# Ranking and writing back tokens in a modulated feed-forward stage: half-width comparisons, a bias put into PSUM by TensorE, residual rows summed on GpSimd

## The reference

```
def _L1_ffn_ref(x, attention_mask, wr, br, w1, b1, w2, b2):
    weights = (jnp.einsum('bsd,do->bso', x, wr) + br)[..., 0]
    k = max(1, int(CAPACITY * s))
    kk = k - 1 if k > 1 else 1
    _, idx = jax.lax.top_k(weights, k)
    sel_idx = idx[:, :kk]
    sel = jnp.take_along_axis(x, sel_idx[:, :, None], axis=1)
    h = jax.nn.gelu(jnp.einsum('bkd,dh->bkh', sel, w1) + b1)
    y = jnp.einsum('bkh,hd->bkd', h, w2) + b2
    w_sel = jnp.take_along_axis(weights, sel_idx, axis=1)
    y = y * w_sel[..., None]
    processed = jnp.zeros_like(x).at[batch_idx, sel_idx].set(y)
    return processed + x

x = x + _L1_ffn_ref(_layernorm(x, axis=-1), ...)
```

## Time and profile before

| | |
|---|---|
| time, median of 3 runs | 4688.07 us (4686.57 to 4688.72) |
| profiled execution, first to last instruction (its span) | 4591.2 us |
| the profiled execution's own time | not recorded apart from its span |
| TensorE matmul busy, share of the span | 3499.2 us, 76% |
| VectorE busy | 2854.1 us, 62% |
| ScalarE busy | 2105.7 us, 46% |
| GpSimd busy | 1802.9 us, 39% |
| the stage `mod_stage` in the span | 2499.3 us to 2699.1 us |

### The profile page before, as it was taken

The page is one execution under the profiler, slowest core; times in us unless marked ns, Lnnn a source line. Parts: engine busy times, 40 slices in busy tenths (PEclk is TensorE's granted clock), DMA queues, the critical chain, the costliest instruction groups (busy, mean ns, idle before and its releaser), DMA issues. The chain is left out here.

```text
span 4591.2 us, 80959 instructions
## 1 busy us (share of the span) xinstructions
PE 3499.2 (76%) x23827; PEld 2132.6 (46%) x23827; DVE 2854.1 (62%) x10855; ACT 2105.7 (46%) x5250; POOL 1802.9 (39%) x2183
## 2 busy tenths in 40 slices
PE   3999995666666638999987867639947788884994
PEld 1333333444444423333345656627736555553663
DVE  5666656555555567777758977832247677763444
ACT  1777773322222216777753236624426555551321
POOL 3555520000000015555456225855545525544444
PEclk8999995555555559999998988869969999996997
DMA  4334318600000014333300012225442000002445
GB/s 130 112 112 118 118 53 368 261 0 0 0 0 0 0 54 126 112 112 111 89 6 2 1 57 71 70 83 153 148 156 80 32 1 20 20 20 85 129 130 162
DMA packets 237349, 378.44 MB, mean 82 GB/s; under 512 B 24832, under 2 KB 157056, under 8 KB 228672
## 3 DMA queue, kind: packets, MB, share of 16 engines
q1 hardware_dynamic: 218688, 337.44, 23.3%
q0 software_dynamic: 18432, 38.31, 2.4%
HBM read 210.70 MB, written 164.95 MB: 82 GB/s over the span
## 5 line engine op out<-in xcount | busy, mean ns | idle before, releaser
L1461 DVE CUSTOM_DVE_ANT_0 mha_seen<-mha_score,mha_mask 128x512 f32<-128x512 f32 x1024 | 684.7, 688 | 378.9 <-PE mha_score L1216 372.9
L1360 ACT ACTIVATE mha_prob<-mha_turned 128x512 f32<-128x512 f32 x1024 | 589.6, 603 | 303.1 <-PE mha_turned L1230 295.9
L1617 PE MATMUL lstm_gates<-lstm_h_part,lstm_w_part 128*128 128x16 f16 x4608 | 277.6, 179 | 327.8 <-DVE lstm_h_part L1832 324.5
L3131 POOL DMA_INDIRECT expert_rows<-expert_y,expert_target x320 | 306.9, 959 | 359.5 <-DVE expert_y L3277 154.6
L1216 PE MATMUL mha_score<-mha_k_rows,mha_q_rows 96*128 96x512 bf16 x1024 | 397.9, 391 | 56.4 <-DMA mha_k_rows<-split_rows 29.5
L1617 PEld LDWEIGHTS lstm_gates<-lstm_h_part,lstm_w_part 128*128 128x128 f16 x4608 | 217.2, 107 | 480.2 <-DVE lstm_h_part L1832 475.5
L1230 PE MATMUL mha_turned<-mha_q_rows,mha_k_rows 99*128 99x512 bf16 x1024 | 389.9, 382 | 8.4 <-ACT mha_turned L1341 6.7
L1564 POOL TENSOR_TENSOR core_mid<-lstm_hist,lstm_per_unit 128x128 f32 x64 | 29.5, 461 | 886.7 <-DVE lstm_hist L1833 886.7
L1704 ACT ACTIVATE lstm_act<-lstm_gates 128x48 f32<-128x48 f32 x512 | 108.0, 211 | 428.6 <-PE lstm_gates L1617 428.6
L1229 PE MATMUL mha_turned<-mha_maskT,core_ident_bf 128*128 128x512 bf16 x768 | 294.8, 384 | 0.3
L3169 PEld LDWEIGHTS expert_out_ps<-expert_w,expert_hid 128*128 128x128 f32 (+1 forms) x2240 | 262.4, 191 | 38.7 <-issue 33.0
(11 more groups left out here) (553 smaller groups left out, 8960.9 us busy)
## 6 DMA issues: line engine op xcount, KB each, us to landing
routed_rows<-lstm_blank SPq DMA_DIRECT2D x66, 1056.0 KB, 27.0
core_params<-adj SPq DMA_DIRECT2D x32, 1024.0 KB, 5.9
gat_adj_raw<-adj SPq DMA_DIRECT2D x32, 1024.0 KB, 5.5
mha_q_rows<-split_rows SPq DMA_DIRECT2D x64, 384.0 KB, 5.3
mha_k_rows<-split_rows SPq DMA_DIRECT2D x64, 384.0 KB, 6.0
expert_x<-routed_rows SPq DMA_DIRECT2D x80, 264.0 KB, 2.8
expert_w<-weights SPq DMA_DIRECT2D x80, 256.0 KB, 3.6
combine_pair<-expert_rows SPq DMA_DIRECT2D x32, 512.0 KB, 4.9
```

The lines of the kernel that those rows point to most:

```text
L1360: act.activation(prob[:, n % RING, :], turned[n % 3][:, :], ACT.Exp, scale=-1.0).then_inc(S["prob_ready"], 1)
L1461: dve.tensor_tensor_reduce(seen[n % 2][:, :], score[n % 2][:, :], mask[1 - s][:, t, :], 1.0, 3e38, ALU.add, ALU.min, low[g][:, t, j:j + 1] ...
L1617: return pe.matmul(out, w[:, g * P:(g + 1) * P], h_part[:, part, :], start=False, stop=stop, skip_group_check=True)
L3131: pool.indirect_dma_start(out=core.y_rows[NUMBER][:, :], out_offset=bass.IndirectOffsetOnAxis(ap=target[q][:, t:t + 1], axis=0), in_=y_buf ...
```

## The change

It touches `mod_stage` alone, in four pieces.

1. The comparisons take only the columns that their mask can leave standing: `earlier` of tile t columns 0 to 128(t+1), `later` of tile t columns 128t to 512.
2. The bias no longer goes through VectorE. Once, at the start of the stage, VectorE cuts it into three bf16 parts that add up to it, and lays them on partitions 0, 32 and 64 of a tile that is otherwise zero (`cut_bias`). TensorE multiplies that tile by a tile of ones and so starts `out_ps` with the bias in all 512 columns; the output matmuls add to it.
3. GpSimd adds the residual rows to the normalised rows (`residual`, into two buffers `base`), as a third pass for each graph. VectorE takes output times coefficient plus `base` straight from `out_ps` into `core.x_res`. The operations into `y` and the sum in `write_x` are gone.
4. The waits that follow from it: `x_taken` (VectorE has taken a graph's output) takes the place of `out_taken`; `base_ready` is new; and TensorE waits for `bias_set` once, behind the first `spread` and ahead of the first hidden tile.

```
+            pool.memset(bias_ones[:, :], 1.0).then_inc(S["bias_set"], 1)
+            def residual(b, s):
+                pool.wait_ge(S["xn_ready"], b + 1)
+                if not isinstance(b, int) or b >= 2:
+                    pool.wait_ge(S["x_taken"], b - 1)
+                apart(pool, core)
+                pool.tensor_tensor(base[s][:, :, :], rows_.xn[b % 3][:, :, :], core.x_res[:, b], ALU.add).then_inc(S["base_ready"], 1)
+            def graph(b, s, first=False, last=False):
+                rows_.normalise(pool, b)
+                residual(b, s)
...
+                if b >= 2:
+                    pe.wait_ge(S["x_taken"], b - 1)
+                pe.matmul(out_ps[s][:, :], bias_ones[:, :], flat(bias_rows[:, :, :]), start=True, stop=False)
                 pe.wait_ge(S["hid_free"], H * (b + 1) + 3)
-                pe.wait_ge(S["out_taken"], b + 1)
...
             spread(0)
+            pe.wait_ge(S["bias_set"], 2)
             each_graph(pe, graph)
...
+            def cut_bias():
+                chain = Chain(dve, S["bias_chain"])
+                left = par("mb2")
+                chain.step(dve.memset(bias_rows[:, :, :], 0.0))
+                for i in range(3):
+                    chain.step(dve.tensor_copy(bias_cut[:, i, :], left))
+                    chain.settle()
+                    if i < 2:
+                        chain.step(dve.tensor_tensor(bias_left[:, :], left, bias_cut[:, i, :], ALU.subtract))
+                        chain.settle()
+                        left = bias_left[:, :]
+                for i in range(3):
+                    row = slice(32 * i, 32 * i + 1)
+                    chain.step(dve.tensor_copy(bias_rows[row, :, :], bias_cut[row, i, :].unsqueeze(1).broadcast_to([1, T, D])))
+                chain.settle()
+                dve.sem_inc(S["bias_set"], 1)
...
-                        chain.step(dve.scalar_tensor_tensor(hits[:, 2 * t + i, :], wrow[:, :], wcol[s][:, t:t + 1],
-                                                            tri[:, t, :], op, ALU.mult, accum_out=count[:, i, t:t + 1]))
+                        chain.step(dve.scalar_tensor_tensor(hits[:, 2 * t + i, lo:hi], wrow[:, lo:hi], wcol[s][:, t:t + 1],
+                                                            tri[:, t, lo:hi], op, ALU.mult, accum_out=count[:, i, t:t + 1]))
...
-                dve.tensor_tensor(y[:, :, :], out_ps[s][:, :].rearrange("p (t d) -> p t d", t=T),
-                                  par("mb2").unsqueeze(1).broadcast_to([P, T, D]), ALU.add).then_inc(S["out_taken"], 1)
+                dve.wait_ge(S["base_ready"], b + 1)
                 for t in range(T):
-                    ins = dve.scalar_tensor_tensor(y[:, t, :], y[:, t, :], coef[:, t:t + 1], rows_.xn[b % 3][:, t, :],
+                    ins = dve.scalar_tensor_tensor(core.x_res[:, b, t, :], out_ps[s][:, t * D:(t + 1) * D], coef[:, t:t + 1],
...
-                write_x(dve, chain, core, b, y[:, :, :], core.x_res[:, b], six)
...
             weigh(0, 0)
+            cut_bias()
+            dve.wait_ge(S["tri_set"], 2)
```

More of the change, by code:

```diff
@@ L2175, in mod_stage @@
         hid = [m.sb(f"hid{s}", [P, H, N]) for s in range(2)]
-        y = m.sb("y", [P, T, D])
+        base = [m.sb(f"base{s}", [P, T, D]) for s in range(2)]
+        bias_left, bias_cut = m.sb("bias_left", [P, D]), m.sb("bias_cut", [P, 3, D], BF16)
+        bias_rows, bias_ones = m.sb("bias_rows", [P, T, D], BF16), m.sb("bias_ones", [P, P], BF16)
         six = m.sb("six", [P, T, 6])
@@ L2231, in graph @@
                         ins = pe.matmul(out_ps[s][:, t * D:(t + 1) * D], hid[s][:, n, t * P:(t + 1) * P],
-                                        par("mw2")[:, n * D:(n + 1) * D], start=(n == 0), stop=(n == H - 1))
+                                        par("mw2")[:, n * D:(n + 1) * D], start=False, stop=(t == T - 1 and n == H - 1))
                 ins.then_inc(S["out_done"], 1)
@@ L2266, in _ @@
             dve.wait_ge(core.params_in[k], 16)
[L2267 to L2269 removed]
+            STEPS = 2 * T
+            def cut_bias():
[14 more added lines that the diff above has]
+                dve.sem_inc(S["bias_set"], 1)
             def weigh(b, s):
```

26 lines of the change are left out of this document (14 added, 12 removed).

## The result

The changed kernel takes 4652.38 us (median of 5 runs, 4650.99 to 4659.14) against 4688.07 us (4683.34 to 4689.94, now 5 runs). The medians differ by 35.7 us. The ratio of the two is 0.9941, with a 95% interval of 0.9920 to 0.9962, which is 17.8 to 37.5 us less. The forecast was 4661.7 us, 26.4 us less. The kernel is faster, and the forecast gain of 26.4 us lies inside that interval; its median lies 9.3 us under the forecast and 3.6 us under the range of 4656 to 4670. The profiled execution took 4651.27 us, with a span of 4649.4 us.

A forecast was written before the change was run, and what follows sets the result against it. VectorE bounds the stage at 11.37 us a graph, then TensorE at 9.4. Loop 27.0 and end 2.4 gain 29.4 us, the start loses 3.0: 26.4 off 4688.07 gives 4661.7 us, 8-in-10 range 4656 to 4670.

The forecast's parts named there:

- The bound: `mod_stage`: VectorE sets the pace at 11.37 us a graph; after the change TensorE does, at 9.4 us.
- the two readings: TensorE's own cycle per graph, read from one graph: 9.38 us or 9.55 us, with 9.4 taken.
- The loop: Spread for graph 1 to that for graph 15: 158.6 us become 131.6 at 9.4 a graph, 27.0 less.
- VectorE: VectorE's cycle per graph: 11.37 less 1.60 (comparisons), 0.71 (L2298) and 1.59 (L202) gives 7.47 us.
- The bias matmul: One added TensorE matmul per graph fits into the 0.34 us wait for ScalarE, cost 0; rival 0.3 a graph, chance 0.08.
- The slack and the pieces: `wide` ready +8.5 us after a spread, asked for at +9.4: slack 0.9; with full-width comparisons +9.4, just in time.
- at about +10.1: When `wide` comes, in us after a spread, if L2298 and L202 (2.3 us) are not removed.
- GpSimd: Its third pass, 1.04 us each, makes about 3.3 us a graph in a 9.4 us cycle; costed at nothing.
- The port rival: GpSimd's three passes hold VectorE's comparisons back 2.0 us a graph; `wide` at +9.8, time 4667.6 us; chance 0.07.
- The start: Stage start: `cut_bias` on VectorE delays TensorE's first hidden tile to 2518.3, a loss of 3.0 us (1.9 to 4.5).
- The end: Spread for graph 15 to the last statistics: 13.7 us become 11.3, 2.4 less.
- From the stage to the time: The 96.9 us around the span stay unchanged, so the stage's 26.4 us come off 4688.07 in full.

## Why the prediction came out as it did

- *The bound.* Right. TensorE is 99% busy, and 9.38 us is its cycle (with the short wait for ScalarE in it); the lower of the two readings (9.38, 9.55) was the true one, and 9.4 was taken. The loop gained 27.3 us, forecast 27.0.
- *VectorE.* Right. From comparison to comparison are 9.39 us, with 0.83 and 1.14 us of waits and 7.4 us of work; forecast 7.47. The price of a column came from a like operation within 1%. The tiles' operations read PSUM at 345 ns, as the earlier trace rows had it.
- *The bias matmul.* Right that it hides in the wait for ScalarE: the output matmuls start as late behind the transposes as before, 0.94 us. The kernel with the bias on VectorE shows that it was not needed, since VectorE had the time for that operation. The prediction had not asked this.
- *The slack and the pieces.* `wide` was foreseen 0.9 us early (0.93 measured), and "just in time" with full comparisons (0.12 early). The step that failed is the last one: "without the removal of L2298 and L202, `wide` would come at about +10.1". It came at 9.77 to 9.79. The sum started from the outputs of the graph before, at +0.2; an engine that is itself the bound does not wait for those. "The narrowing buys little beside the rest" held. It was as true of the rest beside the narrowing, and that was not said.
- *GpSimd.* Nothing held up the steady part: comparisons and statistics last as they do elsewhere. The third pass takes 1.27 us, not 1.04, in all 16 graphs (1.261 to 1.274 us), also where VectorE is idle, so it is the pass itself and no contention. The port rival did not come.
- *The start.* The first hidden tile came 3.8 us later, against 3.0, in the range given (1.9 to 4.5). Of the missing 0.8 us, 0.6 is the first `wide` held up by GpSimd's new pass (0.43 to 1.05 us), which was not in the sum: it had looked for contention in `cut_bias` alone. `cut_bias` itself took 4.0 us with 1.4 of contention in it, while its copies of one row cost 0.3 us each, not 0.43. The term itself was drawn too narrow: it took the start of the first tile for the whole loss and left the rise of the clock at nothing, as something that could go either way. Against the kernel before on chips A and C the start loses 5.2 to 5.3 us. That the profile used had its clock late as well, with first tiles of 6.14 us and not 4.6, hid this; it is luck that the start came out so near.
- *The end.* 2.5 us, forecast 2.4.
- *From the stage to the time.* Here the working was wrong, though it moved no term. It put 96.9 us "around the span". In every profiled execution here only 1.8 to 2.0 us lie around it (4651.27 against 4649.4). The profile of before came from an execution some 95 us shorter than the timed runs, as chip A gives (4590.5), and its stage was a sound basis only because `mod_stage` is alike on all chips. The range was too narrow for the same reason: it took the 2 us between three runs as the noise. The medians differ by 35.7 us where the changed stage gives 26.2 at most. The remaining 9.5 us are not explained by any row: by the medians the comparisons on chips A and C gave 21.5 and 24.5, and the ratio, 0.9941, stands for 27.7, so I take them for the spread between executions, which is argued and not shown. The forecast gain of 26.4 us is near the ratio's 27.7, but on chips A, B and C the change and its variants brought less in the time than in the stage in most comparisons; the step from the stage to the time (that "the change leaves alone" the rest) is not borne out for the graph-attention stage, and it is not disproved.

## What to carry to other kernels

When two engines stand at 11.37 and 9.4 us a cycle, only the first 2 us taken from the slower one count: price each piece of a change both alone and beside the others, since here the narrowing alone brought 21.4 of 24.7 us and the rest alone all of it, and the piece with a cost of its own (the cut bias) was not needed. A loop through two engines may be summed from a hand-over only if the receiver really waits there; otherwise its own cycle is the sum. Work that is done once at the start of a stage belongs in an idle time or behind the first matmuls, and its price includes what it and its neighbours lose beside GpSimd. Where the executions of one kernel have a tail of shorter ones, compare whole sets of runs: the medians hid here that the tail went away.

## What the runs showed of the hardware

The same kernel before took 4593.12 us on chip A (4588.99 to 4601.58, 15 runs), 4703.61 on chip B (4671.43 to 4710.94, 31) and 4708.37 on chip C (4669.51 to 4722.73, 35): 2.5% between chips, against the 0.6% that the change brought. The stages up to and including the changed one agree within some 4 us each on all of them. The difference lies in three late parts: the first experts 367.1 against 383.3 us (A, C), the last attention stage and experts 951.6 against 1017.1, and the graph attention behind the changed stage, in whichever kernel, 354 to 364 us on A, 383 to 389 on B and 358 to 392 on C. The scores of the last attention stage on chip A and chip C, kernel before (columns: count, busy us, mean ns, idle before and its releasers):

```profile
L526 PE MATMUL mha_score<-mha_kT,mha_qT 128*128 128x384 f32 (+3 forms) x508 | 192.4, 464 | 27.5 <-DVE mha_bias L885 27.4
```
```profile
L526 PE MATMUL mha_score<-mha_kT,mha_qT 128*128 128x512 f32 (+3 forms) x512 | 205.5, 488 | 44.2 <-DVE mha_bias L885 38.5 <-POOL mha_kT L431 3.6 <-issue 2.0
```

The same matmuls take 5% longer on C, and the waits in front of them are longer. The granted clock of the last part is 0.90 on chip A and 0.87 to 0.88 on the others. But the first experts' stage is 16 us longer on C at 0.91 than on A at 0.90, so the clock is not all of it. What else differs was not tried and stays open.
